# Last attention of a Flamingo-style stack: the place at which VectorE turns the blocks of a pair of units

## What is computed

```python
def _L3_xattn_ref(x, latents, mask, g1, b1, g2, b2, Wq, Wkv, Wout):
    ...
    heads, dim_head = (16, 64)
    xn = layer_norm(x, g1, b1)
    ln_lat = layer_norm(latents, g2, b2)
    q = ln_lat @ Wq
    kv = jnp.concatenate([xn, ln_lat], axis=1) @ Wkv
    ...
    weight = jnp.einsum('bhld,bhnd->bhln', q * scale, k * scale)
    weight = jnp.where(full_mask[:, None, None, :], weight, neg)
    weight = jax.nn.softmax(weight.astype(jnp.float32), axis=-1).astype(q.dtype)
    out = jnp.einsum('bhln,bhnd->bhld', weight, v)
```

## Time and profile before

| | |
|---|---|
| median of 3 runs | 2944.42 us (2942.79 to 2949.28) |
| the profiled execution | 2945.35 us, span 2943.6 us |
| busy share of the span | PE 84%, PEld 45%, DVE 62%, ACT 40%, POOL 26% |
| stretch of the first last-layer attention, 1235 to 1472 us | PE busy 213.49, DVE 172.43, ACT 136.56, POOL 91.18 |
| the fourth, 2679 to 2900 us | PE busy 205.77, DVE 154.95, ACT 136.13, POOL 91.00 |

### The profile page before, as it was taken

One profiled execution on the slowest core, in us unless ns is written; L12 is line 12 of the kernel. 1 busy time (PEld: TensorE's weight loads), 2 busy tenths in 40 slices (PEclk: granted clock), 3 DMA queues, 4 the chain that ended last, 5 costly groups with the idle time before them and its releaser, 6 DMA issues. The chain is left out here.

```text
span 2943.6 us, 35609 instructions
## 1 busy us (share of the span) xinstructions
PE 2481.0 (84%) x12608; PEld 1335.9 (45%) x12608; DVE 1828.4 (62%) x4072; ACT 1170.7 (40%) x2095; POOL 755.3 (26%) x462
## 2 busy tenths in 40 slices
PE   6888972865888699889899979989988989997996
PEld 2333331323555344545554635554454545463554
DVE  5667745246867474477767357748437875835774
ACT  1433430212323153265544146635325653514662
POOL 1002352520000042043323023414203432402441
PEclk8999985875878799999999999999999999999998
DMA  7411006974200200244320124430023442012442
GB/s 226 136 37 21 11 15 206 316 249 150 87 8 3 106 1 1 87 108 119 97 79 8 73 61 118 116 111 11 8 88 100 116 108 79 1 52 71 110 125 73
DMA packets 112959, 257.06 MB, mean 87 GB/s; under 512 B 36198, under 2 KB 56294, under 8 KB 106762
## 3 DMA queue, kind: packets, MB, share of 16 engines
q1 hardware_dynamic: 93978, 220.26, 24.8%
q10 hardware_dynamic: 12656, 25.97, 3.6%
q0 software_dynamic: 6144, 8.48, 1.0%
HBM read 119.81 MB, written 29.69 MB: 51 GB/s over the span
## 5 line engine op out<-in xcount | busy, mean ns | idle before, releaser
L858 POOL TENSOR_SCALAR pbuf<-pbuf,recip 128x1024 f32<-128x1024 f32 x128 | 364.5, 2848 | 946.0 <-DVE recip L762 946.0
L807 ACT ACTIVATE pbuf<-ps,least 128x1024 f32<-128x1024 f32 x256 | 284.3, 1113 | 295.3 <-DVE least L755 219.5
L755 DVE CUSTOM_DVE_ANT_0 ps<-ps,mask 128x1024 f32<-128x1024 f32 x256 | 307.9, 1244 | 140.2 <-PE ps L687 139.2
L584 POOL TENSOR_SCALAR pbuf<-pbuf,recip 128x512 f32<-128x512 f32 x128 | 200.2, 1576 | 459.7 <-DVE recip L505 459.7
L687 PE MATMUL ps<-kH,qT 64*128 64x512 f32 x1024 | 267.4, 642 | 49.8 <-ACT pbuf L807 47.0
L712 PE MATMUL ps<-work,vh 128*64 128x256 f32 x2048 | 251.9, 390 | 0.0
L555 ACT ACTIVATE pbuf<-ps,least 128x512 f32<-128x512 f32 x256 | 172.7, 686 | 155.6 <-DVE least L495 155.6
L769 DVE STREAM_TRANSPOSE pbuf<-pbuf 128x2048 f32<-128x2048 f32 (+1 forms) x128 | 226.3, 1768 | 0.0
L1554 ACT ACTIVATE early<-ps 128x1536 f32<-128x1536 f32 x86 | 123.9, 1441 | 200.9 <-PE ps L1369 191.7
L1632 DVE TENSOR_REDUCE mh<-ps 128x3 f32<-128x1536 f32 x86 | 150.0, 1744 | 63.8 <-PE ps L1358 61.2
L712 PEld LDWEIGHTS ps<-work,vh 128*64 128x64 f32 x2048 | 138.3, 138 | 95.2 <-issue 36.6
(11 more groups left out here) (371 smaller groups left out, 4054.7 us busy)
## 6 DMA issues: line engine op xcount, KB each, us to landing
work<-pbuf SPq DMA_DIRECT2D x784, 96.0 KB, 2.5
work<-pbuf ACTq DMA_DIRECT2D x240, 96.0 KB, 2.9
early<-in_L_wgu SPq DMA_DIRECT2D x22, 768.0 KB
expert_rows<-zero_rows SPq DMA_DIRECT2D x16, 1024.0 KB, 11.5
yg<-expert_rows SPq DMA_DIRECT2D x16, 1024.0 KB, 6.0
early<-in_L_wd SPq DMA_DIRECT2D x22, 384.0 KB
arena<-in_L_wo SPq DMA_DIRECT2D x8, 1024.0 KB, 8.8
arena<-in_L_wff SPq DMA_DIRECT2D x4, 2048.0 KB, 9.3
```

The source lines that it names most:

```text
L584: nc.gpsimd.tensor_scalar(x, x, recip[:, n % 8:n % 8 + 1], None, mult).then_inc(probs_ready[1], 1)
L755: nc.vector.tensor_tensor_reduce(out=x, in0=x, in1=mask, scale=1.0, scalar=FMAX, op0=add, op1=ALU.min, accum_out=least[:, n % 8:n % 8 + 1])\
L807: nc.scalar.activation(to, x, ACT.Exp, bias=least[:, n % 8:n % 8 + 1], scale=-1.0, accum_out=sums[:, n % 8:n % 8 + 1]).then_inc(taken, 1)
L858: nc.gpsimd.tensor_scalar(unit(n), unit(n), recip[:, n % 8:n % 8 + 1], None, mult).then_inc(pool_divided, 1)
```

## The change

One call moves up by two places in VectorE's loop. For step p, the turn of pair p now stands right behind the first of the two reciprocals, ahead of the copies of slot 2p and ahead of the second reciprocal.

```diff
                 find(2 * p + 2)
                 find(2 * p + 3)
                 invert(2 * p + 2)
+            turn(p)
             keep_jobs(2 * p)
             if p + 1 < N:
                 invert(2 * p + 3)
-            turn(p)
             keep_jobs(2 * p + 1)
```

## The result

The change took 3012.53 us (median of 4 runs, 3006.15 to 3026.39) against 2946.12 (4 runs, 2942.79 to 2949.28): a ratio of 1.0225 [1.0197, 1.0254]. The forecast was 3003 with a range to 3022. The profiled execution took 3008.13 us with a span of 3006.4, 62.8 more than before's span.

The account below looks back on a forecast made before the run. It took a loop through TensorE, VectorE, ScalarE and the transfers as the bound. Changeovers 6.8 + 13.5, opening 18 and closing 20 summed to 58.3 us over 2945.35: forecast 3003 us, range 2984 to 3022.

Parts of the forecast that it names:

- The second key copy: At p % 4 = 2, the long turn of 2.24 us outlasts this copy's 1.19 cover; scores start 1.05 us later.
- V: Start of the first value job's product in a group on TensorE, the zero point for the forecast's times.
- The turn that releases the transfers, and the next exponential: At p % 4 = 3, turn ends at V+15.51 (was V+15.64); next group's exponential starts at V+25.32 (was V+25.38).
- the changeovers: Five groups per batch between opening and closing: +6.8 us in the fourth batch, +13.5 in the other three.
- the gain survives: Rival: the transfer-releasing turn comes 1.18 us earlier in 28 groups, 33 us faster, 2911 us; chance 0.05 (faster).
- The first key copy: At p % 4 = 1 of the next group, the short turn delays this copy; next V at V+28.52, 1.35 us more.
- The closing: End of the first three batches: three products wait longer for copies, plus late scores; 6.7 us each, +20.
- The opening: First group of each batch: late query and key copies delay the second group's scores; +18 us in all.
- 4.5 for each batch: Opening loss per batch: second group's scores 3.7 us later, plus 0.8 from group 1's first key copy.
- The clock rival: Longer TensorE waits bring more half-clock stretches in openings and closings: +23 us on top, 3027 us; chance 0.05.
- The late second reciprocal: At p % 4 = 3 in the first three batches, ScalarE issues transfers up to 1 us later; 0.3 per group.

Follow-up runs that it names:

- step2_only: Changed kernel with the turn moved up only at p % 4 = 2, the long turn ahead of the second key copy: 2993.62 us, ratio 1.0154 to before.
- step3_only: Changed kernel with the turn moved up only at p % 4 = 3, no key or query copy behind it: 2927.37 us, ratio 0.9914 to before.
- short_filler: Changed kernel plus 4 and 2 extra unread TensorE products in each batch's first group: 3016.19 us, ratio 1.0204 to before.
- step1_only: Changed kernel with the turn moved up only at p % 4 = 1, the short turn ahead of the first key copy: 2980.45 us, ratio 1.0100 to before.
- middle: Changed kernel with the turn placed behind the copies of slot 2p, still ahead of the second reciprocal: 2937.56 us, ratio 0.9932 to before.
- step3_middle: Changed kernel with the turn first only at p % 4 = 3, elsewhere between slot 2p's copies and the second reciprocal: 2924.17 us, ratio 0.9899 to before.
- filler: Changed kernel plus 14 and 8 extra unread TensorE products in each batch's first group: 3045.22 us, ratio 1.0304 to before.
- best_filler: step3_middle plus 2, 3 and 2 extra unread TensorE products in each batch's first group: 2917.51 us, ratio 0.9870 to before.

## Why the prediction was right, and where its sizes were off

**The second key copy.** Right. The step said that the long turn of 2.24 us would use up the cover of 1.19 and put the scores at V+9.61. They stand at V+9.58 with a wait of 0.95. step2_only shows that this part by itself is the largest loss.

**The turn that releases the transfers, and the next exponential.** Right in its times. The turn's end was put at V+15.51 and came at V+15.47: its gain was spent on the late scores. step3_only shows the other side: with the scores on time the gain survives, and the changeovers lose 19.3 us. The rival "the gain survives" named 33 us for 28 groups; TensorE's own work stops it sooner. What the step left out is that the transfers need the values products too. Those follow the late scores on TensorE, and end at 2853.00, where the turn ends at 2853.04. SyncE's waits for the turn (us, times, longest), before and after, say how often the turn still was the last to release it:

```profile
SPq L791 <- DVE pbuf L769: 259.3, 61, 35.0
...
SPq L791 <- DVE pbuf L769: 186.4, 21, 38.9
```

Before, it waited for the turn 61 times; in the change 21 times, and otherwise the turn was done when the values products were. There a turn that is earlier still would release nothing sooner.

**The first key copy.** Its sum with the others was right: the period in the fourth batch was predicted as 28.52 and came out at 28.57, the other batches' as 28.85 and (143.81 + 143.46 + 143.05) / 15 = 28.69. In us: +7.0 for 6.8 in the fourth batch and +10.8 for 13.5 in the three others. In four of the fourth batch's five groups V follows V by 28.46 or 28.47, and the exponential waits for its own scores, as the step had it: 2891.84 is 25.29 behind its V, for the 25.32 forecast. The group shown first took 28.98. Its exponential waited for the transfer and came at 2863.38 = V+25.81: it is 10.34 behind the turn's end and not 9.74, most of it by the one issue of 1.69 us. Why that issue took longer stays open.

**The closing.** Right in mechanism, a little small. The windows give +11.3, +4.4, +8.7 and -0.6 for the four batches, 23.7 for the predicted 20. TensorE's timeline at the end of the first batch, which answers to the earlier trace rows:

```profile
1450.04 1.11 PE L872 MATMUL ps<-consts,xn 128*128 128x128 f32 x4 [5.72 <-DVE xnT L2809]
1451.09 3.68 PE L712 MATMUL ps<-work,vh 128*64 128x256 f32 x16
...
1462.37 3.68 PE L3002 MATMUL ps<-arena 128*128 128x128 f32 x16 [2.78 <-DVE cnT L2814]
...
1474.93 2.66 PE L2787 MATMUL ps<-cnT,wk 128*128 128x512 f32 x4 [2.83 <-DVE qT L2782]
```

The three waits grew by 2.48, 1.12 and 2.22, for 2.24, 1.15 and 2.24, and the late scores add a wait of 0.95. TensorE's busy time in this closing grew by 4.51 (40.15 to 44.66) for the same products. Together that is 11.28, the whole of this batch's growth. The longer busy time goes with the clock: the granted clock of the closing fell from 0.96 to 0.88, and behind the first two waits rows of sixteen records took 3.68 us, where the same forms take 1.95 and 2.05 at the higher level. In the second batch the waits grew by 1.37, 1.12, 2.22 and 0.95, but the granted clock rose from 0.93 to 0.97 and the busy time fell by 1.27, so this closing grew by 4.4 only. Over four batches the clock's share is +6.3 (busy 152.95 to 159.29) and the waits' +17.4, for the 20 forecast.

**The opening.** This is the term whose size was off: +18 in the sum, +28.9 measured. The step "4.5 for each batch" was made with the clock as it was, and the text named the rest as left out. TensorE's busy time says how the growth divides: it went from 147.84 to 161.34 us in the four openings, +13.5 for the same products, so the waits gave +15.4. (In the changeovers, with a granted clock of 1.00 in both kernels, the busy time differs by 0.8.) The second group's first scores start 27.94 us behind the first find (2731.77), where they started 23.38 behind it before: 4.6 later, where the step said 3.7. But 1.57 of that is the first value product, which took 3.62 instead of 2.05 behind a wait that grew from 0.91 to 2.63; the waits alone gave 3.0. TensorE's row for it, before and after:

```profile
2689.91 2.05 PE L3002 MATMUL ps<-arena 128*128 128x128 f32 x16 [0.91 <-DVE qT L2782]
...
2742.54 3.62 PE L3002 MATMUL ps<-arena 128*128 128x128 f32 x16 [2.63 <-DVE qT L2782]
```

In the second batch the granted clock of the opening fell from 0.96 to 0.78 and it grew by 9.6 us. short_filler gave back 11.0 of the 28.9, in its profile, by putting work into waits in which TensorE did nothing; that agrees with a share of the clock of this order. The Trainium skill (TensorE: Matmul & The Clock Gate, What's actually happening) says that the array's full rate is something that its activity releases; many rows behind waits of 2 us and more agree, and step1_only shows it in a place where the clock had stood at 1.00 before. But the length of the wait does not decide it by itself: the wait of 2.76 us at the head of the kernel before's four openings was followed by scores of 3.44, 1.99, 2.63 and 3.06 us.

**The clock rival.** It stood at +23 on top, for the opening and closing together, with a chance of 0.05. By the busy time it took +13.5 and +6.3, nearly 20 of the 23, so about what it says did happen, and its chance was too small. That the sum came close all the same is in part luck: the waits gave 15.4, 17.4 and 17.0 (opening, closing, changeovers), 49.8 for the 58.3 forecast, and the clock made up more than the difference. Against the sum of 58.3 the terms were off by +10.9, +3.7 and -2.5 (the changeovers), 12.1 together; the rest of the span gave 7.6 back in the profiled execution, and 62.8 is what is left. The median of the runs lies 4.4 above that execution.

**The excluded ones.** The late second reciprocal, to which the prediction gave 0.3 us for each group of the first three batches, has no price that these runs can tell: middle and step3_middle keep it late and are faster than before.

What stays open: how the effects of the single steps combine (the opening of step1_only was shorter than before, by 3.4 us), why the second closing kept its clock behind the same waits (in filler, whose closings are those of the change, all three stood at 0.97 and took 52.7 to 52.9 us), and whether the filled openings are worth anything beyond the noise of the runs.

## What to carry to other kernels

An idle stretch ahead of an instruction is a place to put work only if what stands behind that instruction has cover for it. Here the turn, moved up by the same two places, gained 0.9% at the one step of four where no key or query copy was queued behind it, and lost 0.9 to 1.5% at each of the others. So before filling a gap of an in-order engine, list each instruction that will stand behind the filler in every phase of the loop, its first and last rounds too, with the time by which its consumer comes for it (here 1.19 us against 2.24); and if TensorE's waits grow by it, give the lower clock a price too: here it was 20 us of the 70 in the windows.

## What was not expected of the hardware

- At V the sixteen records of the value job took 2.05 us behind a wait of 1.26 us, and 3.50 with a granted clock of 0.50 behind one of 2.66 us in step1_only. But behind waits of 2.50 to 2.88 us at the same V in short_filler they took 2.05, and behind waits of 1.43 to 1.57 us in the openings of best_filler the scores took 2.89 to 3.68 instead of 1.99. The same wait of 2.78 us in the closings of the change was followed by 3.68 us in the first batch and by 2.05 in the second. The length of the wait alone does not tell which level the products behind it get.
- A record of a 64-row product costs 0.25 us in the scores, which alternate between the two units of a pair and with them between the two halves of the rows (eight in 1.99), and 0.44 in the filler, which stays with one unit (27 in 11.85), both at a granted clock of 1.00. That the alternation is the cause was not tried by itself. A filler made of the same form of instruction was not of the same price.
